# A convolutional stem with group norm on one Trainium2 core: two patches interleaved in each PSUM bank

## The chip, the cores and the metric

The kernel runs on one core of one Trainium2 chip. A core has five engines that run side by side, each with its own instruction stream: TensorE (PE, matrix multiplies into PSUM), VectorE (DVE), ScalarE (ACT), GpSimd (POOL) and SyncE (SP, which starts DMAs). They wait for each other through semaphores. The metric is the device time of one launch in microseconds (us), as the median of several runs. A matmul puts its 128 output partitions into a bank of PSUM, 512 fp32 columns wide, and VectorE and ScalarE read them from there.

## What is computed

Sixteen images of 3x112x112 are cut into patches of 16x16, 784 in all. Each patch goes through a small residual tower with two group norms, then through a projection to 192 numbers; the 16x49 tokens then pass an attention block and a transformer block ("the tail"), which the change does not touch. Cut to what matters:

```python
x = pixel_values -> patches (784, 3, 16, 16)
x = (x - mean) / (1e-06 + std) / math.sqrt(P)
x = _conv2d(x, conv1_w, conv1_b)            # 3 -> 64 channels, 3x3
residual = x
x = _group_norm(x, gn1_g, gn1_b)            # 32 groups of 2 channels, over 16x16 pixels
x = jax.nn.gelu(x, approximate=False)
x = _conv2d(x, rconv1_w, rconv1_b)          # 64 -> 64, 3x3
x = _group_norm(x, gn2_g, gn2_b)
x = jax.nn.gelu(x, approximate=False)
x = _conv2d(x, rconv2_w, rconv2_b)
x = residual + x
x = _conv2d(x, proj_w, proj_b, stride=P, pad=0)   # to 192
```

The norm of a patch's group is over 2 channels x 256 pixels. The conv biases count in it: the mean is the mean of (y + b), the variance that of (y + b) over both channels.

## The kernel before

**Layout.** Partitions hold 2 halves x 64 channels: the even image rows of a patch are in one half, the odd rows in the other. Free columns hold pixels: `HALF` = 128 per patch (8 rows of 16). A PSUM bank of 512 columns so holds Q = 4 patches, one behind the other. A unit is U = 8 patches, two banks; there are 98 units, in 7 groups of GU = 14.

**Before the loop** (the fold, about the first 269 us of the trace): rconv2 and the projection are both linear, so their weights are multiplied into one set of 128x192 weights per partition (`whi`, `wlo`, fp16 high and low parts). This part uses the same banks `rc` and `c1` and is not changed. ScalarE copies its results out with L366, at a step of 384 bytes in SBUF.

**The loop.** 196 slots, one bank of 4 patches each. In a slot (`emit`, L519) TensorE issues, in this order: 8 matmuls of rconv1 for the slot's bank (`bands`, 18 matmuls of 512 columns in all: fp16 high and low parts of weights and data), the group means of the first norm for a later bank (`means`, L496), 4 more, conv1 of a bank still later (`conv1`, L486: one matmul of 512 columns and one of 64), 3 more, in every second slot the group means of the second norm (both banks of a unit at once), and the last 3. In groups 1 to 6, from the fifth slot on, the projection of the group before is woven in between (`project`, L510 with 384 and L511 with 192 columns, 256 matmuls in 24 slots). Slots in which nothing is woven in are the 28 of group 0 and the first 4 of each other group.

The other engines serve the same ring. VectorE in its slot (L749): `channel_stats` of a bank of c1, four BN_STATS of 128 elements, each giving count, mean and sum of squares for the even and the odd elements (6 numbers); `moments` (L708), four operations, which turn these into mean + bias and mean of squares + eps for each half set; `channel_stats` of a bank of rc; `read_means`, which adds even and odd sets of the group means out of PSUM (a reduce); `split1`, the fp16 split of the activation for rconv1 (`sb_ghl`); `split2`, the low part of the second activation (`sb_arena`). TensorE's `means` multiplies by `grp`, the 128x128 matrix that averages over the four partitions of a group. GpSimd's `norm` (L326) is seven small operations with a power of -0.5 among them; it gives scale and shift (`sb_gsc`, `sb_gsh`) per patch. ScalarE's `gelu1` (L384) and `gelu2_at` (L394) read a bank, one patch of 128 columns each time, and write SBUF; `hi2` rounds to fp16.

Order and waits: each engine's order is written out by hand. A conv1 waits for gelu1 of the bank it overwrites, rconv1 waits for split1 of its input and for gelu2 of the bank it overwrites (s_g2), `means` waits for `moments` (s_ms) and for the reads of the single bank `st` (s_rd), norm waits for read_means. On GpSimd the three norms of two slots follow each other in the order first, second, first.

Before the first conv1 TensorE waits for the fold's last results only (L580 to L583). VectorE widens parameters meanwhile (L685 to L694).

## Time and profile before

| | |
|---|---|
| median of 3 runs | 1872.88 us (1866.81 to 1878.74) |
| the profiled execution: time | 1862.46 us |
| its span | 1860.6 us |
| mean granted TensorE clock | 0.967 of full speed |
| busy: PE / DVE / ACT / POOL | 92% / 72% / 51% / 50% |
| 3528 rconv1 matmuls of 512 columns (L450) | 391 ns mean each |
| 1576 BN_STATS in the loop (L706) | 281 to 283 ns mean each |

How to read it: the span is the time from the first to the last instruction in one profiled execution. Matmuls overlap, so the mean duration of one (391 ns) is longer than the distance to the next; the pace of TensorE is read from the starts of adjacent ones. In a timeline, adjacent instructions of one kind are merged: "x8" with a duration is the time from the first's start to the last's end. A value in square brackets is the idle time before, with what ended it.

### The profile page before, as it was taken

How to read it: one execution, taken by the hardware profiler on the slowest of the kernel's cores; microseconds unless marked ns; L12 is line 12 of the kernel's file. 1: busy time of each engine (PE TensorE's matmuls, PEld its weight loads, DVE VectorE, ACT ScalarE, POOL GpSimd, SP SyncE). 2: the span in 40 equal slices, each digit the busy share in tenths (PEclk: the TensorE clock that was granted, in tenths of full speed). 3: DMA queues.
4: the chain of work that ended last, by engine and by line, in shares of the span. 5: the costliest groups of instructions: out<-in, count | busy, mean ns of one | idle time of the engine just before them, and what ended most of it. 6: DMA issues, size and time to landing. Idle time of an engine off the chain costs nothing. (4 is left out here: it accounts for less than half of the span.)

```text
span 1860.6 us, 35434 instructions
## 1 busy us (share of the span) xinstructions
PE 1711.3 (92%) x8824; PEld 1082.6 (58%) x8824; DVE 1332.0 (72%) x5077; ACT 944.6 (51%) x2114; POOL 937.2 (50%) x2183
## 2 busy tenths in 40 slices
PE   7899978777999999989998999899999979788999
PEld 2344433333577567747775777477657759655657
DVE  8976767777778878878778878778878864348330
ACT  3466654555555555555555555555555550143441
POOL 2000006676676676666676677676677650133410
PEclk9999989999999999999999999999999989787989
DMA  4442332000222121212211221221122237700000
GB/s 147 145 124 85 90 132 81 19 24 20 70 69 67 46 69 48 65 51 67 67 47 48 67 69 41 75 59 56 42 76 69 65 98 194 157 1 1 1 1 14
DMA packets 51109, 124.10 MB, mean 67 GB/s; under 512 B 9167, under 2 KB 26510, under 8 KB 49062
## 3 DMA queue, kind: packets, MB, share of 16 engines
q1 hardware_dynamic: 50982, 122.52, 22.3%
q8 instruction: 66, 1.08, 0.2%
q14 instruction: 61, 0.50, 0.1%
HBM read 102.76 MB, written 19.69 MB: 66 GB/s over the span
## 5 line engine op out<-in xcount | busy, mean ns | idle before, releaser
L450 PE MATMUL rc<-sb_ghl,sb_rws 128*128 128x512 f16 x3528 | 1057.1, 391 | 20.1 <-ACT sb_g2f L399 17.7
L390 ACT ACTIVATE sb_f32q<-c,sb_gsh,sb_gsc 128x128 f32<-128x128 f32 x788 | 296.2, 456 | 346.0 <-POOL sb_gsh L344 346.0
L450 PEld LDWEIGHTS rc<-sb_ghl,sb_rws 128*128 128x128 f16 x3528 | 343.8, 104 | 161.9 <-issue 38.9
L338 POOL TENSOR_TENSOR sb_tmp<-sb_tmp,sb_half_neg 128x4 f32<-128x4 f32 (+1 forms) x296 | 403.3, 1362 | 23.2
L399 ACT ACTIVATE sb_g2f<-rc,sb_gsh,sb_gsc 128x128 f32<-128x128 f32 x784 | 295.6, 467 | 185.6 <-POOL sb_gsh L344 169.9
L333 POOL TENSOR_TENSOR sb_tmp<-sb_mst 128x4 f32<-128x4 f32 (+1 forms) x296 | 72.5, 245 | 518.1 <-DVE sb_mst L722 515.5
L510 PE MATMUL pj<-sb_wall,sb_arena 128*112 128x384 f16 x896 | 299.3, 341 | 10.1 <-DVE sb_arena L746 8.9
L511 PEld LDWEIGHTS pj<-sb_wall,sb_arena 128*112 128x112 f16 x896 | 243.5, 272 | 90.6 <-issue 3.6
L510 PEld LDWEIGHTS pj<-sb_wall,sb_arena 128*112 128x112 f16 x896 | 243.2, 271 | 40.2 <-DVE sb_arena L746 9.0
L746 DVE TENSOR_TENSOR sb_arena<-sb_g2f,sb_arena 128x512 f32 (+1 forms) x196 | 136.6, 697 | 151.3 <-ACT sb_arena L407 137.6
L511 PE MATMUL pj<-sb_wall,sb_arena 128*112 128x192 f16 x896 | 223.5, 249 | 0.0
L450 PE MATMUL rc<-sb_ghl,sb_arena 128*128 128x512 f16 x864 | 204.8, 394 | 19.7 <-DVE sb_ghl L625 19.6
L738 DVE TENSOR_TENSOR sb_ghl<-sb_f32q,sb_ghl 64x64 f16<-64x64 f32 (+1 forms) x591 | 195.2, 359 | 9.4
L706 DVE BATCH_NORM_STATS2 sb_bn<-c 128x6 f32<-128x128 f32 x792 | 174.3, 281 | 6.6 <-issue 5.9
L501 PEld LDWEIGHTS st<-sb_ms,sb_grp 128*128 128x128 f32 x592 | 102.8, 191 | 124.7 <-issue 69.1
L706 DVE BATCH_NORM_STATS2 sb_bn<-rc 128x6 f32<-128x128 f32 x784 | 173.6, 283 | 0.0
L366 ACT ACTIVATE sb_wall<-rc 128x512 f32 (+1 forms) x48 | 120.5, 2510 | 100.3 <-PE rc L450 100.3
L450 PEld LDWEIGHTS rc<-sb_ghl,sb_arena 128*128 128x128 f16 x864 | 81.9, 97 | 139.1 <-issue 31.1
L632 DVE SCALAR_TENSOR_TENSOR sb_arena<-rc,sb_wall 128x512 f32 (+1 forms) x48 | 122.6, 2606 | 51.9 <-ACT sb_wall L366 51.9
L501 PE MATMUL st<-sb_ms,sb_grp 128*128 128x16 f32 (+1 forms) x592 | 101.2, 249 | 57.8 <-DVE sb_ms L718 53.6
L734 DVE CAST sb_ghl<-sb_f32q 64x64 f16<-64x64 f32 (+1 forms) x591 | 137.2, 260 | 6.0 <-ACT sb_f32q L390 3.4
L407 ACT ACTIVATE sb_arena<-sb_g2f 128x512 f32 (+1 forms) x196 | 123.5, 630 | 25.8 <-ACT sb_g2f L399 8.3
(152 smaller groups left out, 1798.2 us busy)
## 6 DMA issues: line engine op xcount, KB each, us to landing
sb_wall<-w_lo SPq DMA_DIRECT2D x28, 1008.0 KB, 4.9
sb_im<-x_planes SPq DMA_DIRECT2D x300, 60.7 KB
sb_wall<-w_lo SPq DMA_DIRECT2D x14, 1056.0 KB, 4.9
sb_im<-x_planes SPq DMA_DIRECT2D x300, 30.3 KB
sb_f32q<-in_proj SPq DMA_DIRECT2D x12, 576.0 KB, 4.2
sb_arena<-in_proj SPq DMA_DIRECT2D x12, 576.0 KB, 4.7
w_lo<-sb_arena SPq DMA_DIRECT2D x1, 6144.0 KB, 17.1
scratch_fold<-sb_wall SPq DMA_DIRECT2D x24, 247.5 KB
```

Of the source, the lines that this page charges most:

```text
L338: ch.did(gp.tensor_tensor(t5, t3, half_neg[:, 0:w], ALU.pow))
L390: ins = nc.scalar.activation(g1f[:, q * Q + m, :], c1[q][:, m * HALF:(m + 1) * HALF], ACT.Gelu, bias=gsh[q][:, m:m + 1], scale=gsc[q][:, m ...
L399: ins = nc.scalar.activation(g2f[:, q * Q + m, :], rc[p][q][:, m * HALF:(m + 1) * HALF], ACT.Gelu, bias=gsh[s][:, q * Q + m:q * Q + m + 1] ...
L407: nc.scalar.activation(g2[:, buf, 0, bass.ds(slot, Q), :], g2f[:, q * Q:q * Q + Q, :], ACT.Copy).then_inc(s_sp2h, 1)
L450: last = nc.tensor.matmul(out, w[:, wp, 3 * t + m, :], v[:, xp, q * Q:q * Q + Q, t:t + 8, m:m + P], start=(n == 0), stop=(n == 17))
L501: nc.tensor.matmul(st[:, 0:4 * wide[s]], grp[:, :], ms[s][:, :, :, :].rearrange("p a b k -> p (a b k)"), start=True, stop=True).then_inc(s ...
L510: yield nc.tensor.matmul(pj[0:G, 0:2 * E], g2[:, b, 0, :, n], both, start=(n == 0), stop=False)
L511: yield nc.tensor.matmul(pj[0:G, 0:E], g2[:, b, 1, :, n], whi[:, n, :], start=False, stop=(n == HALF - 1))
L706: v.bn_stats(bn6[s][:, at + m, :], src[:, m * HALF:(m + 1) * HALF]).then_inc(s_dch[stage_], 1)
L734: ins = v.tensor_copy(hi[half, :, to, :], src[half, :, at, :])
L738: ins = v.tensor_tensor(lo[half, :, to, :], src[half, :, at, :], hi[half, :, to, :], ALU.subtract)
L746: v.tensor_tensor(lo, src, hi, ALU.subtract).then_inc(s_sp2, 1)
```

## The change

In each bank two patches are interleaved: columns 0, 2, 4, ... of the first 256 belong to patch 0 and columns 1, 3, 5, ... to patch 1, and so for patches 2 and 3. BN_STATS gives separate results for even and odd elements, so one call on 256 columns gives three numbers for each of two patches. Matmul outputs of rconv1 and conv1 go through `mixed`, gelus read through `of_pair`. The bias no longer enters per patch: with m the mean and M2 the sum of squares, `moments` forms m(m + 2b) and M2/128 + m(m + 2b) in place, and the groups' averages of b and of b squared + eps, computed once, are added when the means are read. `ms` is gone; the means matmul reads mean and second moment out of `bn6`. `grp` divides by 4 in place of 8.

```diff
-        bn6 = [sb(f"bn6_{s}", [128, w, 6]) for s, w in enumerate(wide)]
-        ms = [sb(f"ms_{s}", [128, 2, w, 2]) for s, w in enumerate(wide)]
-        msq = [sb(f"msq_{s}", [128, w, 2]) for s, w in enumerate(wide)]
+        bn6 = [sb(f"bn6_{s}", [128, w, 3]) for s, w in enumerate(wide)]
+        msq = [sb(f"msq_{s}", [128, w]) for s, w in enumerate(wide)]
...
+            def of_pair(bank, m):
+                return bank[:, :].rearrange("p (a n k) -> p a k n", n=HALF, k=2)[:, m // 2, m % 2, :]
...
-                    ins = nc.scalar.activation(g1f[:, q * Q + m, :], c1[q][:, m * HALF:(m + 1) * HALF], ACT.Gelu,
+                    ins = nc.scalar.activation(g1f[:, q * Q + m, :], of_pair(c1[q], m), ACT.Gelu,
...
-                    ins = nc.scalar.activation(g2f[:, q * Q + m, :], rc[p][q][:, m * HALF:(m + 1) * HALF], ACT.Gelu,
+                    ins = nc.scalar.activation(g2f[:, q * Q + m, :], of_pair(rc[p][q], m), ACT.Gelu,
...
+            def mixed(out):
+                return out.rearrange("p (a n k) -> p a k n", n=HALF, k=2)
...
-                nc.tensor.matmul(c1[q][:, :], w1s[:, :], v[:, q * Q:q * Q + Q, 0:8, 0:P], start=True, stop=True)
-                nc.tensor.matmul(c1[q][0:CH, :].rearrange("p (g n) -> p g n", g=Q)[:, :, 0:P], w1s[:, 0:CH],
+                nc.tensor.matmul(mixed(c1[q][:, :]), w1s[:, :], v[:, q * Q:q * Q + Q, 0:8, 0:P], start=True, stop=True)
+                nc.tensor.matmul(mixed(c1[q][0:CH, :])[:, :, :, 0:P], w1s[:, 0:CH],
...
-                nc.tensor.matmul(st[:, 0:4 * wide[s]], grp[:, :], ms[s][:, :, :, :].rearrange("p a b k -> p (a b k)"),
+                nc.tensor.matmul(st[:, 0:2 * wide[s]], grp[:, :], bn6[s][:, :, 1:3].rearrange("p w k -> p k w"),
...
-                conv = bands(rc[p][q][:, :], rws, ghl[p], q)
+                conv = bands(mixed(rc[p][q][:, :]), rws, ghl[p], q)
...
+            pe.wait_ge(s_wid, 4)
+            nc.tensor.matmul(st[:, 0:4], grp[:, :], bsq[:, :, :].rearrange("p a b -> p (a b)"),
+                             start=True, stop=True).then_inc(s_wid, 1)
+            pe.wait_ge(s_wid, 6)
...
-                ins = v.tensor_scalar(wid[:, s, 0, :], one, 0.0, par[:, 3 * s:3 * s + 1], ALU.mult, ALU.add)
+                v.tensor_scalar(wid[:, s, 0, :], one, 0.0, par[:, 3 * s:3 * s + 1], ALU.mult, ALU.add)
+                v.tensor_scalar(twob[:, s:s + 1], par[:, 3 * s:3 * s + 1], 2.0, None, ALU.mult)
+                v.tensor_copy(bsq[:, s, 0:1], par[:, 3 * s:3 * s + 1])
+                v.tensor_tensor(bsq[:, s, 1:2], par[:, 3 * s:3 * s + 1], par[:, 3 * s:3 * s + 1], ALU.mult).then_inc(s_wid, 1)
+            dve.wait_ge(s_wid, 5)
+            sums = st[:, 0:4].rearrange("p (a b) -> p a b", a=2)
+            v.tensor_copy(bgr[:, :, 0], sums[:, :, 0])
+            v.tensor_scalar(bgr[:, :, 1], sums[:, :, 1], EPS * WS * WS, None, ALU.add).then_inc(s_wid, 1)
+            dve.wait_ge(s_wid, 6)
+            for s in range(2):
+                for k in range(2):
+                    ins = v.tensor_scalar(add[:, s, k, :], one, 0.0, bgr[:, s, k:k + 1], ALU.mult, ALU.add)
...
-                for m in range(Q):
-                    v.bn_stats(bn6[s][:, at + m, :], src[:, m * HALF:(m + 1) * HALF]).then_inc(s_dch[stage_], 1)
+                b6 = bn6[s][:, :, :].rearrange("p (a k) n -> p a (k n)", k=2)
+                for m in range(Q // 2):
+                    v.bn_stats(b6[:, at // 2 + m, :], src[:, 2 * m * HALF:2 * (m + 1) * HALF]).then_inc(s_dch[stage_], 1)
...
-                b6 = bn6[s][:, :, :].rearrange("p g (e k) -> p g e k", e=2)
-                ch.did(v.tensor_scalar(ms[s][:, 0, :, :], b6[:, :, :, 1], par[:, 3 * stage_:3 * stage_ + 1], None, ALU.add))
-                ch.did(v.tensor_scalar(ms[s][:, 1, :, :], b6[:, :, :, 2], 2.0 / HALF, EPS * WS * WS, ALU.mult, ALU.add))
-                dve.wait_ge(s_dch[stage_], ch.at - 1)
-                ch.did(v.tensor_tensor(msq[s][:, :, :], ms[s][:, 0, :, :], ms[s][:, 0, :, :], ALU.mult))
+                mean, m2 = bn6[s][:, :, 1], bn6[s][:, :, 2]
+                ch.did(v.scalar_tensor_tensor(msq[s][:, :], mean, twob[:, stage_:stage_ + 1], mean, ALU.add, ALU.mult))
                 ch.wait()
-                v.tensor_tensor(ms[s][:, 1, :, :], ms[s][:, 1, :, :], msq[s][:, :, :], ALU.add).then_inc(s_ms[stage_], 1)
+                v.scalar_tensor_tensor(m2, m2, 1.0 / HALF, msq[s][:, :], ALU.mult, ALU.add).then_inc(s_ms[stage_], 1)
...
-                v.tensor_reduce(mst[s][:, :, :], st[:, 0:4 * wide[s]].rearrange("p (a b k) -> p a b k", a=2, k=2),
-                                mybir.AxisListType.X, ALU.add).then_inc(s_rd[stage_], 1)
+                v.tensor_tensor(mst[s][:, :, :], st[:, 0:2 * wide[s]].rearrange("p (a b) -> p a b", a=2),
+                                add[:, stage_, :, 0:wide[s]], ALU.add).then_inc(s_rd[stage_], 1)
...
-    o["grp"] = ((i[:, None] == i[None, :]) / 8.0).astype(np.float32)
+    o["grp"] = ((i[:, None] == i[None, :]) / 4.0).astype(np.float32)
```

## Rows read from the trace of the kernel before

**Rows 1.** The page: its span.

```profile
span 1860.6 us, 35434 instructions
```

**Rows 2.** Timeline of TensorE: starts of conv1, group 0 and group 1 (start us, us, what).

```profile
300.31 0.38 PE L492 MATMUL c<-sb_im,sb_w1s 108*128 108x512 f16 x1
...
461.42 0.38 PE L492 MATMUL c<-sb_im,sb_w1s 108*128 108x512 f16 x1
...
486.53 0.38 PE L492 MATMUL c<-sb_im,sb_w1s 108*128 108x512 f16 x1
...
637.21 0.38 PE L492 MATMUL c<-sb_im,sb_w1s 108*128 108x512 f16 x1
```

**Rows 3.** Timeline of TensorE, 700 to 714 us, slots with projection.

```profile
701.87 0.40 PE L501 MATMUL st<-sb_ms,sb_grp 128*128 128x32 f32 x2
702.11 0.38 PE L450 MATMUL rc<-sb_ghl,sb_rws 128*128 128x512 f16 x1
...
703.23 0.32 PE L510 MATMUL pj<-sb_wall,sb_arena 128*112 128x384 f16 x1
703.39 0.60 PE L450 MATMUL rc<-sb_ghl,sb_rws 128*128 128x512 f16 x2
703.83 0.24 PE L511 MATMUL pj<-sb_wall,sb_arena 128*112 128x192 f16 x1
703.91 0.41 PE L450 MATMUL rc<-sb_ghl,sb_rws 128*128 128x512 f16 x1
...
706.83 0.38 PE L492 MATMUL c<-sb_im,sb_w1s 108*128 108x512 f16 x1
...
707.29 0.42 PE L450 MATMUL rc<-sb_ghl,sb_rws 128*128 128x512 f16 x1
...
711.49 0.29 PE L501 MATMUL st<-sb_ms,sb_grp 128*128 128x16 f32 x2
711.63 0.38 PE L450 MATMUL rc<-sb_ghl,sb_rws 128*128 128x512 f16 x1
```

**Rows 4.** Timeline of all engines, 390 to 410 us, slots without projection.

```profile
391.20 1.50 ACT L399 ACTIVATE sb_g2f<-rc,sb_gsh,sb_gsc 128x128 f32<-128x128 f32 x4 [2.28 <-POOL sb_gsh L344]
...
394.34 0.88 DVE L706 BATCH_NORM_STATS2 sb_bn<-c 128x6 f32<-128x128 f32 x4
...
395.26 0.23 DVE L713 TENSOR_SCALAR sb_ms<-sb_bn,sb_par 128x8 f32<-128x8 f32 x1
...
395.52 0.17 DVE L716 TENSOR_TENSOR sb_msq<-sb_ms 128x8 f32<-128x8 f32 x1
...
395.94 0.40 PE L501 MATMUL st<-sb_ms,sb_grp 128*128 128x16 f32 x2 [1.11 <-DVE sb_ms L718]
...
404.09 1.50 ACT L399 ACTIVATE sb_g2f<-rc,sb_gsh,sb_gsc 128x128 f32<-128x128 f32 x4 [2.20 <-POOL sb_gsh L344]
```

**Rows 5.** Groups by line and form: batch-norm statistics.

```profile
L706 DVE BATCH_NORM_STATS2 sb_bn<-c 128x6 f32<-128x128 f32 x792 | 174.3, 281 | 6.6 <-issue 5.9 <-PE c L493 0.6
...
L643 DVE BATCH_NORM_STATS2 sb_g2f<-sb_arena 112x6 f32<-112x256 f32 x21 | 7.0, 409 | 3.1 <-DMA sb_arena<-in_x 3.1
```

**Rows 6.** Groups by line and form: stepped and contiguous accesses (busy us, mean ns, idle before).

```profile
L450 PEld LDWEIGHTS rc<-sb_ghl,sb_rws 128*128 128x128 f16 x3528 | 343.8, 104 | 161.9 <-issue 38.9 <-DVE sb_ghl L738 1.0
...
L511 PEld LDWEIGHTS pj<-sb_wall,sb_arena 128*112 128x112 f16 x896 | 243.5, 272 | 90.6 <-issue 3.6
...
L366 ACT ACTIVATE sb_wall<-rc 128x512 f32 x44 | 110.4, 2510 | 96.0 <-PE rc L450 96.0
L407 ACT ACTIVATE sb_arena<-sb_g2f 128x512 f32 x168 | 105.9, 630 | 24.9 <-ACT sb_g2f L399 8.3
```

**Rows 7.** Timeline of TensorE, 268 to 305 us.

```profile
280.01 3.60 PE L450 MATMUL rc<-sb_ghl,sb_rws 128*128 128x512 f16 x8 [0.91 <-DVE sb_ghl L738]
283.40 0.45 PE L501 MATMUL st<-sb_ms,sb_grp 128*128 128x16 f32 x2
```

**Rows 8.** By window: busy us of PE, PEld, DVE, ACT, POOL; granted clock; DMA.

```profile
280.00:283.40 3.40, 3.39 (x9) 1.34 (x10) 1.47 (x8) 1.18 (x4) 0.00 (x0) 0.50 1.22 463
```

More of the change, by code:

```diff
@@ L108, in build_front @@
         wid = sb("wid", [128, 2, 3, U])
+        bsq = sb("bsq", [128, 2, 2])
+        bgr = sb("bgr", [128, 2, 2])
+        add = sb("add", [128, 2, 2, U])
+        twob = sb("twob", [128, 2])
         zeros = sb("zeros", [128, U])
@@ L754, in slot @@
                     channel_stats(0, N1[q], c1[q], 0)
-                    moments(0, N1[q], 7 * (k + 2) + 4)
+                    moments(0, N1[q], 3 * (k + 2) + 2)
                     if n2:
@@ L764, in slot @@
                     if q == 0 and n2:
-                        moments(1, N2[1 - p], 11 * (u - 1) + 8)
+                        moments(1, N2[1 - p], 5 * (u - 1) + 4)
                     if not (first and p == 0) and not (first and p == 1 and q == 0):
@@ L794, in _ @@
             channel_stats(0, 0, c1[0], 0)
-            moments(0, 0, 4)
+            moments(0, 0, 2)
             dve.wait_ge(s_c1, 3)
             channel_stats(0, 1, c1[1], 0)
-            moments(0, 1, 11)
+            moments(0, 1, 5)
             read_means(0, 0, 0)
@@ L812, in _ @@
             channel_stats(1, N2[1], rc[1][1], Q)
-            moments(1, N2[1], 11 * (UNITS - 1) + 8)
+            moments(1, N2[1], 5 * (UNITS - 1) + 4)
             read_means(1, N2[1], UNITS - 1)
```

## Prediction

> **What bounds the kernel now.** I read the page first: the profiled execution has a span of 1860.6 us [rows 1] and a time of 1862.46 us. The page calls TensorE busy for nearly all of it, but ends of matmuls are modelled, so I don't use that share and read the pace from starts.
>
> The whole middle of the kernel is a loop of 196 slots (98 units, two banks each), and each slot has one conv1. So the starts of conv1 (L492) measure a slot. In group 0, where no projection is woven in, 25 slots take 161.11 us, 6.44 us each; in group 1, 24 slots with projection take 150.68 us, 6.28 us each [rows 2]. The slots with *more* TensorE work are the shorter ones, so the two kinds have different limits, and a change is worth something else in each.
>
> Next, the timeline of TensorE in slots with projection. A 512-column conv matmul is followed by the next after 0.22 us (703.39 to 703.83 holds two), a projection pair adds 0.16 and 0.08 us, conv1 takes 0.46 us in its two matmuls, the group means 0.24 us when they have 32 columns and 0.14 us when they have 16 [rows 3]. One slot holds 18 conv matmuls (3.96 us), one conv1 (0.46), on average 5.33 projection pairs (1.28), one narrow means in each slot and one wide in every second (0.26): 5.96 of 6.28 us. These 144 slots (24 in each of six groups) are bound by TensorE.
>
> In a slot without projection the same sum is 3.96 + 0.46 + 0.26 = 4.68 us, far below 6.44. The full timeline of two such slots shows a ring instead: gelu2 on ScalarE at 391.20, VectorE's statistics of c1 at 394.34, the moments at 395.26, the means on TensorE at 395.94, then GpSimd's two norms, and gelu2 again at 404.09, 12.89 us later, which is two slots [rows 4]. Here no engine is full; the chain is the limit. There are 52 such slots: 28 in group 0, and 4 at the head of each of the other six, which I take at the 6.28 us of their neighbours, since no step of mine hangs on it.
>
> **The change, part by part.**
>
> *Statistics.* Four BN_STATS of 128 elements become two of 256. Four take 0.88 us with 0.28 us for one, so they start 0.20 us apart [rows 4, 5]. A 256-element one took 409 ns against 281 [rows 5], 0.13 us more, so two take 0.33 + 0.41 = 0.74 us: 0.14 us saved per call, two calls a slot. In the ring only one call of each two slots lies on the path; elsewhere VectorE has idle time, and it's worth nothing.
>
> *Moments.* Four operations become two, both dependent. From the first to the start of the means took 0.68 us; from the third operation (395.52), so for two dependent operations, 0.42 us [rows 4]. Saved: 0.26 us per call. One of these lies in the ring. read_means changes a reduce for an addition of the same output width: nothing.
>
> *Group means.* Columns halve: 16 to 8 and 32 to 16. The step from 32 to 16 columns is worth 0.10 us [rows 3], so from 16 to 8 I take 0.05 us. The moving operand now steps 12 bytes inside bn6, which no row prices: the saving is 0 to 0.10 us a slot, I take 0.10 where TensorE binds.
>
> *New preparation.* Once, ahead of the first conv1, TensorE now waits for s_wid 6: six widenings, two scalings, eight operations for the bias squares and doubles, one matmul and two more on VectorE. At 0.13 us apart (395.26 to 395.52 is two) [rows 4] 18 operations are 2.3 us, with the trip to TensorE about 3, of which VectorE's part was before it already ahead of the first statistics: +2.5 us. Nothing hides it. The wait has conv1 and everything of TensorE behind it, once.
>
> *GpSimd and DMAs.* Norms keep their seven operations and their inputs' form; no DMA moves.
>
> *The interleave itself.* This is the term that decides. All conv and conv1 outputs now go to the bank at a step of two fp32 (8 bytes), where every output was contiguous before; 18 matmuls of 512 columns and conv1 in each slot. ScalarE reads its 128 elements at that step. No row of before has a stepped output of TensorE, so I bound it. Below: nothing, 0.22 us stays. Above: other engines' stepped accesses. ScalarE writing 128x512 at a step of 384 bytes took 2510 ns against 630 ns for the contiguous copy, 4.0 times; TensorE's weight load at a step of 256 bytes took 272 ns against 104, 2.6 times [rows 6]. Four times is 0.87 us a matmul. Between, TensorE has a pace that the trace shows: where the granted clock was 0.50, the lower of its two levels (1.2 of 2.4 GHz), eight conv matmuls start at 280.01 us and the next instruction at 283.40, 0.42 us apart; 512 columns at 1.2 GHz are 0.427 us, which I use [rows 7, 8]. I take 0.427 us: every stepped access that the trace has is slowed, the step here is the smallest of them, and two times is between none and the 2.6 of TensorE's own stepped load.
>
> The row shows only that a stepped access costs TensorE 2.6 times on its read side [rows 6]. The Trainium skill, "PSUM — Partial Sum Buffer", section Specifications (TRN2), says that PSUM's lines are 8 bytes and that "any non-contiguous AP slows matmuls significantly"; "Advanced Engine Details and Errata", section PSUM Cachelines, adds that each two consecutive elements should be contiguous. Two fp32 fill such a line, so a step of two would use half of every line; by an estimate from that page a matmul would take twice its time, which is the same 0.43 us. No row of this trace shows a stepped matmul output. By the row of no penalty the sum would be 1839 us, by the rule some 2530 us.
>
> Slots with projection: 18 x (0.427 - 0.22) = 3.73 us, conv1 0.21 + 0.03, together 3.97; some of the 0.32 us of bubbles is absorbed, so +3.9 us, x 144 = +562 us. Slots without: 18 x 0.427 = 7.69, conv1 0.70, means 0.26, so 8.65 us. That is more than the ring's 6.44 per slot, so TensorE becomes the limit here too: (8.65 - 6.44) x 28 = 62 us and (8.65 - 6.28) x 24 = 57 us. Means: 0.10 x 196 = -20 us. Preparation +2.5 us. The ring's savings are worth nothing here. Sum: 1862.5 + 562 + 62 + 57 - 20 + 2.5 = 2526 us. The median shown, 1872.88, is 10 us above the profiled execution, so I say **2536 us**. ScalarE's stepped reads have no row either: a slot has two gelus of 1.50 us and a copy of 0.63 us [rows 4, 6]; at once to twice the gelus' time that is 3.6 to 6.6 us of a slot of 8.65 or more, so nothing in this case; I take once.
>
> **The rivals.**
>
> *No penalty, shorter chain (ends faster).* TensorE writes stepped columns at full rate. Then the ring loses 0.14 + 0.26 + 0.05 = 0.45 us of its 12.89 per two slots, x 26 = 12 us, and 144 slots lose 0.10 us, 14 us; +2.5: 1862.5 - 12 - 14 + 2.5 = 1839, with the 10 us 1849 us. For it: each term has a row. Against it: every stepped access in [rows 6] is dear. It decides as soon as a conv matmul stays below 0.23 us.
>
> *No penalty and the gain is hidden.* The means are no shorter (the 12-byte step eats the fewer columns) and the ring hands its 0.45 us to GpSimd's norms: 1862.5 + 2.5 - 0 to 12, with the 10 us 1863 to 1875 us. For it: 144 of 196 slots are TensorE's, and VectorE's saved time lies beside idle time there.
>
> *A dearer step.* Each stepped column costs four, as on ScalarE [rows 6]: 0.87 us a matmul, 19 matmuls, +12.4 us in 144 slots and about +10.6 us in 52: near 4200 us. Against it: that step is 384 bytes, this one 8.
>
> *A part penalty*, between 0.23 and 0.42 us a matmul (only the start of a run, or only accumulation): 1900 to 2450 us.
>
> **How the numbers follow.** Doubled matmuls 0.57 (own range 2430 to 2620), part penalty 0.05, dearer step 0.05, no penalty with the gain 0.19, no penalty hidden 0.14. Slower by over 1% is 0.57 + 0.05 + 0.05 = 0.67. The gain's 1849 us is 1.3% under 1873, so its 0.19 splits 0.14 faster and 0.05 same; same is 0.14 + 0.05 = 0.19. About 1% is what a measurement of this kernel can tell from no change. Both signs hold much of the chance, so the range must span them: 1840 us (the gain with all its terms) to 2620 us leaves out the dearer step and the edges, about 0.12.
>
> **What would show each step.** Starts of two adjacent L450 matmuls: 0.43 us apart at full granted clock if I am right, 0.22 if not. A slot with projection near 10.1 us, one without near 8.7, with TensorE's waits on sb_ms and sb_g2f gone. Statistics: half as many rows, about 0.41 us each. The two moments operations 0.2 us apart. The narrow means: 0.10 us to the next conv. If slots of group 0 become shorter than 6.44 us, the forecast is wrong as a whole, since the penalty is its only large term. If the matmuls double and group 0 is still above 9 us, a chain that I called slack has become the limit.

## The result and the profile after

The changed kernel takes 2514.3 us (median of 4 runs, 2512.95 to 2527.22) against 1871.22 us for the kernel before, a ratio of 1.3447 (95% interval 1.3383 to 1.351): 34% slower. The profiled execution of the kernel after took 2514.44 us with a span of 2512.5 us, against the 1860.6 us of [rows 1].

The page of the kernel after: span, busy time of each engine, and three of its groups (count | busy us, mean ns of one | idle time before, and what ended most of it):

```profile
span 2512.5 us, 33782 instructions
...
PE 2430.3 (97%) x8826; PEld 1280.3 (51%) x8826; DVE 1247.4 (50%) x3709; ACT 945.6 (38%) x2114; POOL 882.5 (35%) x2183
...
L461 PE MATMUL rc<-sb_ghl,sb_rws 128*128 128x512 f16 x3528 | 1758.2, 611 | 0.4 <-DVE sb_ghl L762 0.4
...
L746 DVE TENSOR_TENSOR sb_mst<-st,sb_add 128x8 f32<-128x8 f32 (+1 forms) x296 | 50.1, 169 | 736.3 <-PE st L512 736.3
...
L733 DVE BATCH_NORM_STATS2 sb_bn<-rc 128x6 f32<-128x256 f32 x392 | 149.5, 423 | 166.2 <-PE rc L461 156.0
```

The reader is to see that the work removed is gone (33782 instructions for 35434; the statistics are half as many) and that the other engines now wait for TensorE (VectorE directly, for the means in `st` and for the bank `rc`; GpSimd and ScalarE behind it), whose rconv1 matmuls grew from 391 to 611 ns. The idle time of TensorE's own group is 0.4 us in 3528 instructions.

The duration of one matmul overlaps with its neighbours, so the pace is again read from starts. Timeline of TensorE in the kernel after (start us, us, what), one slot of group 0 without projection, then a stretch of group 1 with projection:

```profile
542.93 0.63 PE L503 MATMUL c<-sb_im,sb_w1s 108*128 108x512 f16 x1
543.50 0.24 PE L504 MATMUL c<-sb_im,sb_w1s 108*64 108x64 f16 x1
543.67 6.18 PE L461 MATMUL rc<-sb_ghl,sb_rws 128*128 128x512 f16 x14
549.65 0.33 PE L512 MATMUL st<-sb_bn,sb_grp 128*128 128x8 f32 x2
549.83 1.88 PE L461 MATMUL rc<-sb_ghl,sb_rws 128*128 128x512 f16 x4
...
563.92 0.37 PE L521 MATMUL pj<-sb_wall,sb_arena 128*112 128x384 f16 x1
564.13 1.02 PE L461 MATMUL rc<-sb_ghl,sb_rws 128*128 128x512 f16 x2
564.95 0.29 PE L522 MATMUL pj<-sb_wall,sb_arena 128*112 128x192 f16 x1
```

Fourteen matmuls fill 543.67 to 549.65 us, 5.98 us, 0.427 us each, where [rows 3] has 0.22. Two of them between projection matmuls take 0.82 us (564.13 to 564.95), 0.41 each, but the projection matmul ahead of them takes 0.21 us (563.92 to 564.13) where [rows 3] has 0.16 for the same one, written contiguously in both kernels. So at a change of bank a part of the price only shows in the neighbour.

The slots, from the starts of conv1 (L503), group 0 and then group 1:

```profile
318.34 0.63 PE L503 MATMUL c<-sb_im,sb_w1s 108*128 108x512 f16 x1
...
534.23 0.63 PE L503 MATMUL c<-sb_im,sb_w1s 108*128 108x512 f16 x1
...
569.72 0.59 PE L503 MATMUL c<-sb_im,sb_w1s 108*128 108x512 f16 x1
...
807.51 0.63 PE L503 MATMUL c<-sb_im,sb_w1s 108*128 108x512 f16 x1
```

25 slots take 215.89 us, 8.64 each, and 24 take 237.79 us, 9.91 each, against 6.44 and 6.28 [rows 2]. The four slots at the head of the next group went from 6.28 to 8.87 us. The extra is 3.63 x 144 = 523 us in slots with projection, 2.19 x 28 = 61 us in group 0 and 2.59 x 24 = 62 us at the heads, together 646 us. The span grew by 651.9 us.

One stretch that was not expected to say anything, the first slots at half clock (granted 0.50, as in [rows 8]):

```profile
276.05 1.03 PE L503 MATMUL c<-sb_im,sb_w1s 108*128 108x512 f16 x1 [0.32 <-DVE sb_bgr L715]
277.02 0.32 PE L504 MATMUL c<-sb_im,sb_w1s 108*64 108x64 f16 x1
```

Conv1's 512 columns take 0.97 us here, where the same matmul of the kernel before took 0.52 us at the same clock (269.61 to 270.13). The stepped output costs nearly twice, 1.87 times, at half clock too.

### The profile page after: what moved, and what is told of

Same layout as the page of the kernel before. It is cut to its first block and busy times, and to the rows that moved or that the text cites. A ratio compares the mean times of both kernels' runs of the same rounds, so it can differ in the third digit from the quotient of the medians.

```text
span 2512.5 us, 33782 instructions
## 1 busy us (share of the span) xinstructions
PE 2430.3 (97%) x8826; PEld 1280.3 (51%) x8826; DVE 1247.4 (50%) x3709; ACT 945.6 (38%) x2114; POOL 882.5 (35%) x2183
## 5 line engine op out<-in xcount | busy, mean ns | idle before, releaser
L461 PE MATMUL rc<-sb_ghl,sb_rws 128*128 128x512 f16 x3528 | 1758.2, 611 | 0.4 <-DVE sb_ghl L762 0.4
L461 PEld LDWEIGHTS rc<-sb_ghl,sb_rws 128*128 128x128 f16 x3528 | 427.8, 127 | 428.2 <-issue 198.2
L341 POOL TENSOR_TENSOR sb_tmp<-sb_tmp,sb_half_neg 128x4 f32<-128x4 f32 (+1 forms) x296 | 414.1, 1399 | 23.2
L746 DVE TENSOR_TENSOR sb_mst<-st,sb_add 128x8 f32<-128x8 f32 (+1 forms) x296 | 50.1, 169 | 736.3 <-PE st L512 736.3
L522 PEld LDWEIGHTS pj<-sb_wall,sb_arena 128*112 128x112 f16 x896 | 255.6, 285 | 189.7 <-issue 183.4
L521 PE MATMUL pj<-sb_wall,sb_arena 128*112 128x384 f16 x896 | 331.1, 376 | 9.2 <-DVE sb_arena L770 8.9
L521 PEld LDWEIGHTS pj<-sb_wall,sb_arena 128*112 128x112 f16 x896 | 246.2, 275 | 75.0 <-issue 65.4
L522 PE MATMUL pj<-sb_wall,sb_arena 128*112 128x192 f16 x896 | 255.4, 285 | 0.0
L733 DVE BATCH_NORM_STATS2 sb_bn<-rc 128x6 f32<-128x256 f32 x392 | 149.5, 423 | 166.2 <-PE rc L461 156.0
L512 PEld LDWEIGHTS st<-sb_bn,sb_grp 128*128 128x128 f32 x592 | 126.7, 215 | 92.3 <-issue 80.3
L733 DVE BATCH_NORM_STATS2 sb_bn<-c 128x6 f32<-128x256 f32 x396 | 150.9, 423 | 17.8 <-PE c L504 6.6
L647 DVE SCALAR_TENSOR_TENSOR sb_arena<-rc,sb_wall 128x512 f32 (+1 forms) x48 | 122.3, 2608 | 51.2 <-ACT sb_wall L369 51.2
```

Of the source, the lines that this page charges most:

```text
L341: ch.did(gp.tensor_tensor(t5, t3, half_neg[:, 0:w], ALU.pow))
L461: last = nc.tensor.matmul(out, w[:, wp, 3 * t + m, :], v[:, xp, q * Q:q * Q + Q, t:t + 8, m:m + P], start=(n == 0), stop=(n == 17))
L512: nc.tensor.matmul(st[:, 0:2 * wide[s]], grp[:, :], bn6[s][:, :, 1:3].rearrange("p w k -> p k w"), start=True, stop=True).then_inc(s_st[st ...
L521: yield nc.tensor.matmul(pj[0:G, 0:2 * E], g2[:, b, 0, :, n], both, start=(n == 0), stop=False)
L522: yield nc.tensor.matmul(pj[0:G, 0:E], g2[:, b, 1, :, n], whi[:, n, :], start=False, stop=(n == HALF - 1))
L733: v.bn_stats(b6[:, at // 2 + m, :], src[:, 2 * m * HALF:2 * (m + 1) * HALF]).then_inc(s_dch[stage_], 1)
```

## Where the loss is: the layout alone

All experiments are told by the slots as well as by the time, since the slots say which kind of work paid. The columns are: a slot of group 0 (no projection), a slot of group 1 with projection, a slot at the head of group 2, and the time from the first to the last conv1 in the profiled execution. What lies behind the last conv1 is nearly the same code in all of them and took 336.2 to 352.9 us without any order by layout, so differences of some us between two times say less than a slot does, which repeats to about 0.01 us between kernels that should be alike.

| kernel | group 0 | projection | head | loop us |
|---|---|---|---|---|
| before | 6.44 | 6.28 | 6.28 | 1247.3 |
| after | 8.64 | 9.91 | 8.87 | 1892.8 |
| layout alone, step 2 | 8.64 | 9.91 | 8.88 | 1896.9 |
| layout alone, step 4 | 8.64 | 9.91 | 8.88 | 1894.2 |
| after, contiguous banks | 6.09 | 6.12 | 6.09 | 1209.3 |
| the same, wide means | 6.10 | 6.12 | 6.10 | 1209.5 |
| the same, four statistics | 6.22 | 6.13 | 6.20 | 1216.9 |
| the same, four moments | 6.29 | 6.25 | 6.13 | 1232.3 |
| the same, both | 6.43 | 6.29 | 6.26 | 1245.3 |
| alternating pairs | 6.17 | 6.92 | 6.16 | 1329.5 |
| alternating pairs, other order | 6.17 | 6.92 | 6.16 | 1333.0 |
| runs of 4 | 6.38 | 6.54 | 6.05 | 1279.1 |
| runs of 16 | 6.45 | 6.28 | 6.28 | 1246.5 |

**The kernel before with the interleaved layout, and nothing else of the change.** Statistics, moments, means and preparation stay as they were; four BN_STATS read one patch each at a step of two.

```diff
-nc.tensor.matmul(c1[q][:, :], w1s[:, :], ...)
+nc.tensor.matmul(mixed(c1[q][:, :]), w1s[:, :], ...)     # likewise rconv1
-v.bn_stats(bn6[s][:, at + m, :], src[:, m * HALF:(m + 1) * HALF])
+v.bn_stats(bn6[s][:, at + m, :], of_patch(src, m))       # likewise the gelus
```

> The kernel before with the interleaved layout alone: rconv1 and conv1 write at a step of two fp32, ScalarE and VectorE read each patch at that step; statistics (four of 128), moments, means and preparation stay as before. Theory (the stepped output of the matmuls is the whole loss): adjacent conv matmuls 0.43 us apart, a slot without projection about 8.7 us, 2525 us (2500 to 2550), that is the changed kernel's 2514 plus up to 20 us for the wider means. Rival (the new means, which read bn6 at a step of 12 bytes, or the shorter chain of moments carry part of the loss): the time lies at least 50 us below the changed kernel's, under 2464 us.

It takes 2516.42 us, ratio 1.3507 (1.3439 to 1.3576). Its matmuls:

```profile
L456 PE MATMUL rc<-sb_ghl,sb_rws 128*128 128x512 f16 x3528 | 1761.3, 612 | 0.4 <-DVE sb_ghl L744 0.4
...
L712 DVE BATCH_NORM_STATS2 sb_bn<-c 128x6 f32<-128x128 f32 x792 | 175.3, 285 | 16.2 <-PE c L499 6.1
```

That is the whole loss: 612 ns like the 611 of the kernel after, and every kind of slot equals its slot to 0.01 us. The readers of PSUM pay next to nothing: BN_STATS at a step of two takes 285 ns where the contiguous one took 281 [rows 5], and a gelu of c1 456 ns with or without the step. And since this kernel still has means of 16 and 32 columns, the narrower ones brought the kernel after nothing while TensorE is the limit.

**All four patches of a bank interleaved, a step of four fp32.** This separates "a second column of the same 8 bytes" from "the further, the dearer".

```diff
-return out.rearrange("p (a n k) -> p a k n", n=HALF, k=2)
+return out.rearrange("p (n k) -> p k n", n=HALF, k=4)
```

> As the run with the layout alone, but all four patches of a bank are interleaved: a step of four fp32 (16 bytes). Everything else is as before. Theory A (a column alone in its 8 bytes costs two columns' time, however far the next is): matmuls 0.43 us apart, the same 2525 us as with a step of two. Theory C (the price grows with the step): over 0.5 us apart, over 2800 us; at four times 0.87 us and about 4200 us.

2519.82 us, ratio 1.3526 (1.3458 to 1.3594), and the same matmul row:

```profile
L456 PE MATMUL rc<-sb_ghl,sb_rws 128*128 128x512 f16 x3528 | 1758.6, 611 | 0.4 <-DVE sb_ghl L744 0.4
```

The price does not grow from 8 to 16 bytes: it is two times once, and the "dearer step" rival, taken from ScalarE's 384 bytes in SBUF [rows 6], has no hold on this write.

## What the rest of the change is worth

**The kernel after with contiguous banks.** One BN_STATS can still serve two patches if only its *read* interleaves them: the access pattern takes column n of the first patch, column n of the second, column n + 1 of the first, and so on. TensorE and the gelus go back to contiguous patches.

```diff
-nc.tensor.matmul(mixed(c1[q][:, :]), w1s[:, :], ...)     # likewise rconv1 and the gelus
+nc.tensor.matmul(c1[q][:, :], w1s[:, :], ...)
-v.bn_stats(b6[:, at // 2 + m, :], src[:, 2 * m * HALF:2 * (m + 1) * HALF])
+v.bn_stats(b6[:, at // 2 + m, :],
+           src[:, 2 * m * HALF:2 * (m + 1) * HALF].rearrange("p (k n) -> p n k", k=2))
```

> The changed kernel with contiguous banks: matmuls write and ScalarE reads as before, and only BN_STATS walks its 256 columns alternately (one of the first patch, one of the second), so that the even and odd results still belong to one patch each. New moments, means and preparation stay. Theory: matmuls 0.22 us apart again, BN_STATS as in the changed kernel (0.42 us), the ring of slots without projection 0.45 us shorter in two slots, the means up to 0.10 us cheaper in a slot: 1840 to 1862 us, ratio to before 0.984 to 0.995. Rival 1 (a stepped read of PSUM costs VectorE as a stepped write costs TensorE): BN_STATS near 0.7 us, the ring longer, 1865 to 1900 us. Rival 2 (the narrow means save nothing): 1858 to 1866 us, all of the gain in slots without projection.

1830.8 us (6 runs, 1820.23 to 1838.79) against 1863.08, ratio 0.9834 (0.9798 to 0.987). It is 1.7% faster than the kernel before; the change was worth having, only its layout in PSUM was not needed for it. The expectation of 1840 to 1862 us was missed on the good side, and what it said of the means was wrong, as is shown below. Its groups:

```profile
L461 PE MATMUL rc<-sb_ghl,sb_rws 128*128 128x512 f16 x3528 | 1054.5, 390 | 22.6 <-ACT sb_g2f L406 20.2
...
L733 DVE BATCH_NORM_STATS2 sb_bn<-c 128x6 f32<-128x256 f32 x396 | 149.4, 419 | 6.0 <-issue 5.5
```

Matmuls are back at 390 ns, and the interleaving read costs VectorE nothing (419 ns; 423 in the kernel after, where the same 256 elements lie contiguous). The ring of slots without projection, timeline of all engines:

```profile
387.93 1.50 ACT L406 ACTIVATE sb_g2f<-rc,sb_gsh,sb_gsc 128x128 f32<-128x128 f32 x4 [2.26 <-POOL sb_gsh L347]
...
391.06 0.76 DVE L733 BATCH_NORM_STATS2 sb_bn<-c 128x6 f32<-128x256 f32 x2
...
391.86 0.22 DVE L740 SCALAR_TENSOR_TENSOR sb_msq<-sb_bn,sb_twob 128x4 f32<-128x4 f32 x1
...
392.34 0.39 PE L512 MATMUL st<-sb_bn,sb_grp 128*128 128x8 f32 x2 [0.78 <-DVE sb_bn L742]
...
393.10 0.27 POOL L336 TENSOR_TENSOR sb_tmp<-sb_mst 128x4 f32<-128x4 f32 x1 [2.79 <-DVE sb_mst L746]
...
395.52 0.52 POOL L345 TENSOR_TENSOR sb_tmp<-sb_tmp,sb_gsc 128x4 f32<-128x4 f32 x1
...
396.12 0.20 POOL L347 TENSOR_TENSOR sb_gsh<-sb_wid,sb_tmp 128x4 f32<-128x4 f32 x1
...
400.11 1.50 ACT L406 ACTIVATE sb_g2f<-rc,sb_gsh,sb_gsc 128x128 f32<-128x128 f32 x4 [2.18 <-POOL sb_gsh L347]
```

And the three rows of the kernel before that answer to the GpSimd ones, beside [rows 4]:

```profile
396.84 0.28 POOL L333 TENSOR_TENSOR sb_tmp<-sb_mst 128x4 f32<-128x4 f32 x1 [3.25 <-DVE sb_mst L722]
...
399.26 0.73 POOL L342 TENSOR_TENSOR sb_tmp<-sb_tmp,sb_gsc 128x4 f32<-128x4 f32 x1
...
400.07 0.20 POOL L344 TENSOR_TENSOR sb_gsh<-sb_wid,sb_tmp 128x4 f32<-128x4 f32 x1
```

Two slots take 12.18 us for 12.89. Piece by piece: statistics to moments 0.80 for 0.92, moments to means 0.48 for 0.68, means to the norm's first operation 0.76 for 0.90, the norm to its last operation 3.02 for 3.23, and from there to gelu2 3.99 for 4.02. Of the first two I had said 0.40 (0.32 measured); of the next two, 0.35 us, only 0.05 for the narrower means. The norm's seven operations are unchanged, and the 0.21 us that it gained lie in one of them, the sixth (L342, now L345): it takes 0.73 us from 399.26 before and 0.52 us from 395.52 now, and 0.20 in a norm that runs beside no split (393.11). Both times it runs beside VectorE's `split2` (0.69 us from 399.25 before, from 395.29 now) and ends 0.05 to 0.06 us after it. So GpSimd seems to be held until VectorE is done; that was not tested.

In slots with projection the gain is not spread. Before, from the second slot of group 1 on, slots of 5.92 to 6.09 us alternate with slots of 6.41 to 6.63 us, and the longer ones are those with the wide means of the second norm; with contiguous banks the short ones are unchanged and the long ones take 6.18 to 6.27. The timeline of TensorE around the wide means, before and then after with contiguous banks:

```profile
713.96 0.41 PE L450 MATMUL rc<-sb_ghl,sb_rws 128*128 128x512 f16 x1
714.45 0.40 PE L501 MATMUL st<-sb_ms,sb_grp 128*128 128x32 f32 x2
```

```profile
712.40 0.41 PE L461 MATMUL rc<-sb_ghl,sb_rws 128*128 128x512 f16 x1
712.67 0.39 PE L512 MATMUL st<-sb_bn,sb_grp 128*128 128x16 f32 x2
712.91 0.38 PE L461 MATMUL rc<-sb_ghl,sb_rws 128*128 128x512 f16 x1
```

From the conv matmul to the means it was 0.49 us and is 0.27; from the means to the next conv matmul it is 0.24 us as in [rows 3], with half the columns. So TensorE had been waiting there for the moments of 16 columns, part of what I called bubbles. The summary of its waits says the same, from 320 to 1530 us, over both kinds of slot (us in total, times, longest), before and after with contiguous banks:

```profile
PE st L501 <- DVE sb_ms L718: 48.1, 72, 2.9
```

```profile
PE st L512 <- DVE sb_bn L742: 27.5, 44, 2.3
```

**Are the fewer columns worth anything?** The same kernel, with means as wide as before (each column twice).

```diff
-nc.tensor.matmul(st[:, 0:2 * wide[s]], grp[:, :], bn6[s][:, :, 1:3].rearrange("p w k -> p k w"), ...)
+nc.tensor.matmul(st[:, 0:4 * wide[s]], grp[:, :],
+                 bn6[s][:, :, 1:3].rearrange("p w k -> p k w").unsqueeze(1).broadcast_to((128, 2, 2, wide[s])), ...)
```

> The kernel with contiguous banks and interleaved reads (1831 us), with the group means' moving operand read twice (16 and 32 columns as before the change, the second half unused). In that kernel the step from the means to the next conv stayed 0.14 and 0.24 us although the columns were halved. Theory 1 (the means' cost doesn't hang on the number of columns in this range): steps stay, 1826 to 1836 us. Theory 2 (halving was worth 0.05 and 0.10 us and the 12-byte step of the moving operand ate it): steps 0.19 and 0.34 us or more, 1840 to 1855 us.

1831.89 us, ratio 0.9831 (0.979 to 0.9872), against 0.9834 without them; the loop differs by 0.2 us of 1209. Between 8 and 32 columns the number of columns costs nothing that can be measured, and neither does the step of 12 bytes with which the means read bn6: the gaps are 0.14 and 0.24 us as in [rows 3].

**Statistics in four calls.** Each BN_STATS of 256 becomes two of 128. The first of each pair is written beside, so half the pixels are left out of the statistics; the number and length of operations are those of before.

```diff
-v.bn_stats(b6[:, at // 2 + m, :], pair)
+v.bn_stats(b6x[s][:, at // 2 + m, :], pair[:, 0:HALF // 2, :])
+v.bn_stats(b6[:, at // 2 + m, :], pair[:, HALF // 2:, :])
```

> The kernel with contiguous banks and interleaved reads (1831 us), with each BN_STATS of 256 elements cut into two of 128, of which only the second is used (half of the pixels is left out of the statistics). Theory (what the joint statistics save is 0.14 us of VectorE's time per call, and it reaches TensorE only where TensorE waits for moments): BN_STATS 0.28 us each, 0.88 us for four; slots without projection 0.07 to 0.15 us longer, of the slots with projection only the ones with the wide means longer, by up to 0.15 us: 1838 to 1850 us. Rival (VectorE isn't on any path, and the gain is all from the moments): 1828 to 1835 us.

1834.54 us, ratio 0.9862 (0.9816 to 0.9908). The time alone would not tell it from the 1830.8 us without the edit; it lies in the range of the rival (1828 to 1835) and below that of the theory. The slots do tell: 6.22 for 6.09 in group 0 and 6.20 for 6.09 at the heads, but 6.13 for 6.12 with projection. The loop loses 7.6 us of the 38 that contiguous banks had gained.

**Moments in four operations.** Two more operations of the old form are put ahead of the two, into buffers that nobody reads.

```diff
+v.tensor_scalar(mx0[:, 0:wide[s]], mean, par[:, 3 * stage_:3 * stage_ + 1], None, ALU.add)
+v.tensor_scalar(mx1[:, 0:wide[s]], m2, 2.0 / HALF, EPS * WS * WS, ALU.mult, ALU.add)
 ch.did(v.scalar_tensor_tensor(msq[s][:, :], mean, ...))
```

> The kernel with contiguous banks and interleaved reads (1831 us), with two more small VectorE operations at the head of each moments, whose results aren't used, so that it has four operations as before the change. Theory (moments carry the larger part of the gain, both in the ring and in the wait of TensorE for the wide means): moments 0.2 to 0.26 us longer, 1843 to 1857 us, and this rise and that of the run with four statistics add up to the 32 us between before and this kernel. Rival (the small operations run in the shadow of a wait): 1828 to 1835 us.

1844.63 us, ratio 0.9901 (0.9865 to 0.9938). The loop loses 22.9 us: the moments are three quarters of what the two edits return one by one, and they do it in both kinds of slot (6.29 for 6.09 and 6.25 for 6.12 us). The expectation that the two rises add up to the whole 32 us did not come true: by the medians they are 4 and 14 us, by the loop 30.5 of 38.

**Both at once,** with half the pixels left out as above.

> The kernel with contiguous banks and interleaved reads, with both four statistics of 128 and four moments operations put back (half of the pixels is left out of the statistics). Alone, the first lengthened the time from the first to the last conv1 by 8 us and the second by 23 us, of 38 us between that kernel and before. Theory (both lie in one chain and together give all of it back): first to last conv1 1245 to 1250 us as before (1247), 1858 to 1870 us. Rival (a third part of the change, the sum read with an addition in place of a reduce or the narrower means, carries the missing 7 us): 1240 us, about 1856 us or less.

1867.37 us against 1866.94, ratio 1.0004 (0.9981 to 1.0027); the loop is 1245.3 us, before it was 1247.3. So statistics and moments are nearly the whole gain, 36.0 of 38 us of the loop, a little more together than the 30.5 of the two alone. The bias constants, the addition that replaces the reduce, and the narrower means bring 2 us at most.

## What exactly is dear in the write

A step of two doubles the matmul and a step of four does no more. Is it any break in the addresses, or the lone column?

**Patches alternate by pairs of columns.** The kernel before, with a bank laid out as two columns of patch 0, two of patch 1, two of 2, two of 3, and again: 8 bytes written, then a jump of 32.

```diff
+return out.rearrange("p (n k w) -> p k n w", n=HALF // 2, k=4, w=2)
```

> The kernel before with another layout alone: the four patches of a bank alternate by pairs of columns, so that a matmul writes two neighbouring fp32 (8 bytes) and then jumps by 32 bytes; ScalarE and VectorE read each patch that way. Theory A (what costs is a written column that stands alone in its 8 bytes): conv matmuls 0.22 us apart, 1855 to 1880 us, no change to before. Theory B (any output that isn't contiguous is slow): 0.43 us apart, near the 2520 us of the steps of two and of four. A part price (0.25 to 0.40 us apart) would say that the jump itself costs and is shared by two columns.

1954.64 us against 1865.3, ratio 1.0496 (1.0454 to 1.0537). The loss is a seventh of the step's, and neither of the two theories is right for all matmuls. (The same idea with two patches in place of four, a jump of 16 bytes, gave no result; only the jump of 32 bytes is measured.) The mean of the matmuls is 443 ns, which mixes two kinds. Timeline of TensorE in a slot with projection, from conv1 on:

```profile
764.72 0.95 PE L456 MATMUL rc<-sb_ghl,sb_rws 128*128 128x512 f16 x2
765.49 0.27 PE L517 MATMUL pj<-sb_wall,sb_arena 128*112 128x192 f16 x1
765.59 0.77 PE L456 MATMUL rc<-sb_ghl,sb_rws 128*128 128x512 f16 x2
766.20 0.32 PE L516 MATMUL pj<-sb_wall,sb_arena 128*112 128x384 f16 x1
766.37 0.60 PE L456 MATMUL rc<-sb_ghl,sb_rws 128*128 128x512 f16 x2
766.80 0.24 PE L517 MATMUL pj<-sb_wall,sb_arena 128*112 128x192 f16 x1
766.88 0.38 PE L456 MATMUL rc<-sb_ghl,sb_rws 128*128 128x512 f16 x1
767.10 0.32 PE L516 MATMUL pj<-sb_wall,sb_arena 128*112 128x384 f16 x1
```

The last three (766.37 to 767.10) take 0.22 us each, the price of a contiguous write; the two before 765.49 take 0.77 us together, 0.385 each, and the next two 0.61, one of either kind. Over the slot 12 of 18 are at 0.22 and 6 near 0.385 (0.389 between two of their kind, 0.36 to 0.375 at a change of bank). The 18 are two rounds of nine; within a round the horizontal shift m of the 3x3 kernel goes 0, 1, 2, three matmuls each, and it is the three with m = 1 that are dear. Their moving operand starts one fp16 element into the row, an odd place; the write is the same for all.

**The same with the shifts in the order 1, 0, 2.** This tells the odd start from the place in the sequence.

```diff
-for m in range(3):
+for m in (1, 0, 2):
```

> The layout with pairs of columns, with the three horizontal shifts of rconv1's input issued in the order 1, 0, 2 in place of 0, 1, 2 (same 18 matmuls, another order). With pairs, 12 of a slot's 18 conv matmuls were 0.22 us apart and 6 were 0.38 us: the fourth to sixth and the thirteenth to fifteenth, which are the ones whose moving operand starts one fp16 element to the right (shift 1). Theory (the price hangs on the odd start of the moving operand): the slow ones are now the first to third and the tenth to twelfth, time the same 1945 to 1960 us. Rival (it hangs on the place in the sequence, a queue that fills): the slow ones stay fourth to sixth and thirteenth to fifteenth.

1949.36 us, ratio 1.0447 (1.0394 to 1.05), the same slots. The dear matmuls moved with m = 1 to the head of each round. The first matmul of a bank:

```profile
808.82 0.55 PE L456 MATMUL rc<-sb_ghl,sb_rws 128*128 128x512 f16 x1
809.18 0.35 PE L516 MATMUL pj<-sb_wall,sb_arena 128*112 128x384 f16 x1
```

0.36 us for one now (808.82 to 809.18), at a place where the order 0, 1, 2 has 0.22 (766.88 to 767.10). So it hangs on the odd start.

**Runs of 4 and of 16 columns.** The same layout with longer runs between the jumps.

```diff
+return out.rearrange("p (n k w) -> p k n w", n=HALF // 4, k=4, w=4)      # or // 16 and w=16
```

> The same layout test with runs of four columns: each patch's four neighbouring columns (16 bytes) stand together, then the output jumps by 64 bytes. Theory (columns are delivered in pairs, and a pair costs double only where its two columns fall on both sides of a jump; with an odd start every pair did so in the run with pairs, here every second one): even starts 0.22 us, odd starts about 0.30 us apart, loss half of the 92 us of the pairs: 1895 to 1920 us. Rival (any jump slows an odd-start matmul as a whole): 1945 to 1960 us.

1895.3 us against 1866.94, ratio 1.0157 (1.0116 to 1.0198), at the lower end of what was expected. The dear ones are down to 0.31 us (808.08 to 808.69 holds two):

```profile
808.08 0.78 PE L456 MATMUL rc<-sb_ghl,sb_rws 128*128 128x512 f16 x2
808.69 0.34 PE L516 MATMUL pj<-sb_wall,sb_arena 128*112 128x384 f16 x1
```

> The same with runs of sixteen columns, one row of the image: the output jumps by 256 bytes after each 64 bytes. Theory (a pair costs double only across a jump): one pair in eight for odd starts, so 0.22 to 0.24 us apart, 1858 to 1880 us, no measurable change. Rival (any output that isn't contiguous is slow, by the number of its dimensions): above 1900 us.

1866.2 us, ratio 1.0006 (0.9983 to 1.003), slots and loop as before, 391 ns a matmul. Breaks between runs of 16 cost nothing that can be measured. But two of its matmuls with an odd start take 0.49 us (704.99 to 705.48), and so they do in the kernel before, where the output is contiguous: 0.49 us for two with m = 1 (707.71 to 708.20), 0.44 us for two with an even start (708.66 to 709.10). First runs of 16, then before:

```profile
704.99 0.65 PE L456 MATMUL rc<-sb_ghl,sb_rws 128*128 128x512 f16 x2
705.48 0.24 PE L517 MATMUL pj<-sb_wall,sb_arena 128*112 128x192 f16 x1
```

```profile
707.71 0.65 PE L450 MATMUL rc<-sb_ghl,sb_rws 128*128 128x512 f16 x2
708.20 0.24 PE L511 MATMUL pj<-sb_wall,sb_arena 128*112 128x192 f16 x1
...
708.66 0.60 PE L450 MATMUL rc<-sb_ghl,sb_rws 128*128 128x512 f16 x2
709.10 0.24 PE L511 MATMUL pj<-sb_wall,sb_arena 128*112 128x192 f16 x1
```

So an odd start has a price of its own, an eighth (0.245 for 0.218 us), which the prediction did not have. The expectation above puts up to 0.24 us down to one broken pair in eight, but the kernel before shows the same without any break. The usual gaps (medians over the loop, in us) between the starts of two matmuls of the same kind, away from any change of bank, are:

| output | even start | odd start |
|---|---|---|
| contiguous (before) | 0.218 | 0.245 |
| runs of 16 | 0.218 | 0.245 |
| runs of 4 | 0.218 | 0.309 |
| runs of 2 | 0.218 | 0.389 |
| step of 2 or 4 | 0.429 | 0.429 |

What fits all of them is this: the array takes its columns in pairs, aligned on the moving operand, and a pair costs more when its two columns do not land side by side. One row of the image is 16 columns. From an even start that is 8 pairs; from an odd start it is a single column, 7 pairs and a single one, 9 in all, and 9/8 of 0.218 is the 0.245 us. With a step of two or four every pair is broken, and the price is two times. With runs of two or more none is broken while the start is even. With an odd start 7 pairs of a row are broken in runs of two, 3 in runs of four and none in runs of sixteen. The extra over 0.245 is 0.144, 0.064 and 0.000 us, in the proportion of 7, 3 and 0. The gaps are shown; the pairs are an inference from them. What stays open is why a broken pair costs only three quarters of a whole one here (0.0206 us for each of a row's broken pairs, where one of 8 pairs is 0.027): with a full one, runs of two would by this estimate take 0.44 and runs of four 0.33 us. It is not tested either why the slots without projection are shorter with runs of two and of four than before (6.17 and 6.38 for 6.44 us), although TensorE has more to do in them.

The Trainium skill, "PSUM — Partial Sum Buffer", section Specifications (TRN2), gives a line of 8 bytes, and the steps of two and four, which leave one column in each such line, do cost twice (0.429 for 0.218 us). But its "any non-contiguous AP slows matmuls significantly" is too wide by these runs: pairs with an even start and runs of 16 are not contiguous and cost nothing.

## The prediction, step by step

**What bounds the kernel.** Right in both kinds of slot, with two omissions. I read the slots with projection as bound by TensorE's own work and let 0.32 us of each stand as bubbles. Only half of that is waiting: the 0.22 us that I took for every conv matmul holds for 12 of 18, and the six with an odd start take 0.245, which is 0.16 us a slot. The other half is TensorE's wait for the moments of the wide means, about 0.31 us once in two slots, 48.1 us in 72 waits from 320 to 1530 us in both kinds of slot (the lines are above), which I had not priced. With contiguous banks this wait is nearly gone, and the slot takes 6.12 us, my 5.96 and the 0.16 of the odd starts. A TensorE that needs 9.91 us waits for nobody: its matmuls' waits for the moments fell to 3.4 us in 2 waits (320 to 2100 us).

**The interleave.** Its size of 0.427 us per matmul is what was measured, and so is the mechanism that the layout is the only large term (the layout alone gives the same slots). The reason I gave for the number was weaker than the number. I took it from TensorE's pace at half clock [rows 7, 8] as a value between none and 2.6 times, and the rows that gave the 2.6 and the 4.0 differ in more than the step (112 columns for 128; a source in PSUM for one in SBUF), so they bound it loosely. At half clock the stepped write is nearly doubled again (0.97 for 0.52 us), so the price follows the clock; that the two figures agree comes of both being a factor of two, and as far as it rests on the half clock it is luck.

**Slots with projection.** This is the term that was mis-sized: +3.9 us, x 144 = 562 predicted, +3.63 us and 523 measured. The failed step is "some of the 0.32 us of bubbles is absorbed". I let 0.07 us be absorbed, and all 0.32 went, for two reasons: the wait for the wide means (0.16 us a slot) vanished behind a TensorE that is the limit by far, and the odd starts (0.16 us a slot) cost nothing more once every column costs double (0.429 us from either start). My own terms, 5.96 + 3.97 = 9.93 us, were the length of a slot without either, and the slot became 9.91. Conv1's two matmuls take 0.70 us in these slots, as in the sum (0.74 in slots without projection). The conv matmuls at a change of bank take about 0.39 us and the projection matmuls 0.04 more each than before, which cancels.

**Slots without.** 8.65 predicted, 8.64 measured, +62 and +61 us. At the heads of groups 57 predicted, 62 measured (8.87 us a slot; a slot is measured from conv1 to conv1, so the last of the four already holds part of the projection).

**Means.** -20 us predicted, 0 measured. The step that failed is reading the difference between 0.24 and 0.14 us in [rows 3] as the price of 16 columns. The wide means stand at another place in the slot than the narrow ones; with 8 and with 32 columns the next conv matmul came as soon (the run with wide means). In the kernel after, the narrow means take 0.18 us (549.65 to 549.83) where I had said 0.10. Why the wide ones take 0.10 us more is open; it is not their columns.

**Preparation.** +2.5 us predicted. From the start of the fold's last low part on VectorE (L632, now L647; 266.94 and 271.26 us) to the first conv1 (269.61 and 276.05) it was 2.67 us and is 4.79, so +2.1.

**The sum.** 2526 us against 2514.4 for the profiled execution: 39 too many in the projection slots, 20 too few from the means, 5 too few at the heads, and about 4 too few ahead of the loop, whose first conv1 came 6.4 us later for the 2.5 of the preparation (the rest lies in the fold, which the change does not touch). That the misses partly cancel is luck. The 10 us that I added, since the median of before stands above its profiled execution, did not come: the kernel after has its median at its profiled time.

**The rivals.** "No penalty, shorter chain" was run as the kernel after with contiguous banks. I gave it 1839 us for the profiled execution, which took 1820.23, and 1849 for the median, which is 1830.8. The direction and the ring are right, with 0.71 us for two slots where I had 0.45. In the projection slots there was a gain of 0.16 us, beside the 0.10 predicted, for another reason: the moments came earlier, and the columns count for nothing. "The gain is hidden" is excluded for that kernel by its interval (0.9798 to 0.987): VectorE's time did not lie idle in all 144 slots, since TensorE waited for it once in each two.

## What to carry to other kernels

Put the access pattern where it is free: here the interleave cost 34% on TensorE's write into PSUM and nothing on VectorE's read out of it, for the same statistic. When a term makes one engine the limit by far, build the new slot from the bare sum of its starts, and drop every wait that the old slot held. Take the pace of an operation for each of its forms: here a third of the conv matmuls was an eighth slower by where its input starts, and that was half of what looked like waiting in the old slot. Price an operation from the gap between its own start and the next, and check that nothing else differs before a difference of two gaps is put down to size.

## What the runs showed of the hardware that was not expected

- Matmul outputs of 512 fp32 columns at a step of 8 and of 16 bytes are paced alike, 0.43 us for 0.22. At the lower clock conv1 shows nearly the same factor, 0.97 for 0.52 us.
- With a contiguous output a matmul whose fp16 moving operand starts at an odd element of a row of 16 takes 0.245 us, from an even one 0.218.
- A write in pairs of columns with a jump of 32 bytes costs nothing (0.218 us) from an even start and 0.389 us from an odd one. In runs of four the odd ones take 0.309 us, in runs of 16 the 0.245 of the contiguous output.
- Reads of PSUM at a step are next to free on the two engines that do it here: a gelu of 128 columns takes 457 ns at a step of two for 456 contiguous, BN_STATS of 128 takes 285 for 281, and BN_STATS of 256 alternating between two patches 128 columns apart takes 419 for 423.
- Group means with 8, 16 and 32 columns of fp32 cost TensorE the same, contiguous or read at a step of 12 bytes.
